# Scalar-tensor-tensor in place of tensor-tensor for three vector operations of a routing stage

## The reference

```python
def _L0_ffn_ref(hidden_states, rms_w, gate_w, w13, w2, sw_gate, sw_up, sw_down):
    H, I, E, K, CAP = 256, 128, 64, 2, 256
    x = _rmsnorm(hidden_states, rms_w).reshape(-1, H)
    logits = x @ gate_w.T
    topk_w, topk_ids = top_k(softmax(logits), K)
    topk_w = topk_w / sum(topk_w)
    ... # sort the 2T choices by expert, at most CAP per expert in its buffer
    xb = buf[:, :CAP]
    g, u = split(einsum('ech,ehf->ecf', xb, w13))
    yb = einsum('eci,eih->ech', silu(g) * u, w2)
    moe_out = ...  # weighted rows back to their tokens
    shared = silu(x @ sw_gate) * (x @ sw_up) @ sw_down
    return moe_out + shared + residual

x = x + 0.5 * ffn(layernorm(x))
x = x + attn(layernorm(x))     # MLPs of width 1024, causal mixing of 1024 tokens
x = x + 0.5 * ffn(layernorm(x))
```

## Time and profile before

| what | value |
|---|---|
| three timed runs | 2141.43, 2149.87, 2153.97 us (median 2149.87) |
| the profiled execution | 2137.34 us, its span 2135.6 us |
| granted TensorE clock, mean | 0.977 of full speed |
| busy share of the span: PE, DVE, ACT, POOL | 92%, 62%, 51%, 52% |
| stage `dispatch`: start of its last VectorE operation (L496) | 189.19 us |

### The profile page before, as it was taken

The page is one execution under the profiler, slowest core; times in us unless marked ns, Lnnn a source line. Parts: engine busy times, 40 slices in busy tenths (PEclk is TensorE's granted clock), DMA queues, the critical chain, the costliest instruction groups (busy, mean ns, idle before and its releaser), DMA issues.

```text
span 2135.6 us, 32644 instructions
## 1 busy us (share of the span) xinstructions
PE 1970.7 (92%) x11134; PEld 1676.3 (78%) x11134; DVE 1319.4 (62%) x3475; ACT 1084.4 (51%) x1989; POOL 1117.6 (52%) x1251
## 2 busy tenths in 40 slices
PE   6996899599999999999999999999999977898987
PEld 4665888578888888888888888888888865788854
DVE  5996666455566576576575575665665543555568
ACT  6873666444445455454454454454454534455652
POOL 5875667353255546545645645545545326466610
PEclk9998999899999999999999999999999989999998
DMA  8434899790032022121220210110100302688787
GB/s 283 150 119 144 276 295 299 251 308 27 1 99 80 21 99 65 36 94 35 70 87 23 89 40 21 60 40 21 60 11 21 126 11 70 220 276 304 277 281 270
DMA packets 236407, 270.09 MB, mean 126 GB/s; under 512 B 25489, under 2 KB 186322, under 8 KB 236242
## 3 DMA queue, kind: packets, MB, share of 16 engines
q1 hardware_dynamic: 207570, 200.79, 29.0%
q0 software_dynamic: 28672, 67.22, 9.5%
HBM read 150.35 MB, written 117.57 MB: 125 GB/s over the span
## 4 chain that ended last, share of the span: by engine, by line
PE 66%; DVE 6%; issue 3%; ACT 3%; POOL 1%; another core or an unknown queue 1%; DMA 0%; ACTq 0%; DVEq 0%; POOLq 0%
PE attention_ring L1997 22%; PE attention_acc L2027 14%; PE attention_acc L2017 8%; PE attention_acc L2264 3%; PE attention_acc L2252 2%; DVE attention_hid_l L1712 2%; PE attention_work L2090 2%; PE attention_ring L2252 2%; PE attention_work L2110 2%; PE attention_work L2106 2%; PE attention_work L2073 2%; PE attention_ring L2206 2%; PE attention_ring L2239 1%; PE attention_work L1985 1%; PE attention_work L2047 1%
## 5 line engine op out<-in xcount | busy, mean ns | idle before, releaser
L1712 DVE TENSOR_TENSOR attention_hid_l<-attention_gelu,attention_hid_h 128x512 fp32r<-128x512 f32 x384 | 286.0, 745 | 467.6 <-ACT attention_gelu L1351 270.1
L1348 ACT ACTIVATE attention_hid_h<-attention_ring,home_b 128x512 fp32r<-128x512 f32 x384 | 264.3, 688 | 540.3 <-PE attention_ring L1997 475.7
L1351 ACT ACTIVATE attention_gelu<-attention_ring,home_b 128x512 f32<-128x512 f32 x384 | 261.7, 682 | 0.0
L1997 PE MATMUL attention_ring<-attention_n_t_h,home_w_h 128*128 128x512 f32 x512 | 204.0, 398 | 1.6 <-DVE attention_n_t_l L1704 1.6
L2027 PE MATMUL attention_acc<-attention_hid_h,home_w_h 128*128 128x512 f32 x512 | 201.2, 393 | 2.9 <-DVE home_room L1729 1.3
L1997 PE MATMUL attention_ring<-attention_n_t_h,home_w_l 128*128 128x512 f32 x512 | 199.8, 390 | 0.0
L2027 PE MATMUL attention_acc<-attention_hid_l,home_w_h 128*128 128x512 f32 x512 | 199.6, 390 | 0.0
L1997 PE MATMUL attention_ring<-attention_n_t_l,home_w_h 128*128 128x512 f32 x512 | 199.5, 390 | 0.0
L2027 PE MATMUL attention_acc<-attention_hid_h,home_w_l 128*128 128x512 f32 x512 | 199.3, 389 | 0.0
L1190 POOL DMA_INDIRECT home_room<-expert_rows,routing_slots x128 | 139.0, 1086 | 93.9 <-issue 54.1
L1326 POOL DMA_INDIRECT token_rows<-home_room,attention_gelu x128 | 128.7, 1005 | 99.0 <-ACT home_room L1447 64.2
(11 more groups left out here) (309 smaller groups left out, 5259.6 us busy)
## 6 DMA issues: line engine op xcount, KB each, us to landing
experts_w<-in_L_ffn_w SPq DMA_DIRECT2D x64, 256.0 KB
expert_rows<-experts_y SPq DMA_DIRECT2D x64, 256.0 KB
slot_rows<-const_zeros SPq DMA_DIRECT2D x16, 1024.0 KB
token_rows<-const_zeros SPq DMA_DIRECT2D x16, 1024.0 KB
home_room<-in_L_ffn_w SPq DMA_DIRECT2D x64, 256.0 KB
home_room<-slot_rows SPq DMA_DIRECT2D x64, 256.0 KB
final_y_rows<-token_rows SPq DMA_DIRECT2D x32, 512.0 KB, 6.5
dispatch_x_in<-in_L_attn_x SPq DMA_DIRECT2D x16, 512.0 KB, 5.6
```

What stands on the lines that cost most here:

```text
L1348: act.activation(hid[n % PARTS][0][:, :], ring[n % RING][:, :], ACT.Gelu, bias=b1[:, m, c:c + 1])
L1351: act.activation(gelu[n % GELUS][:, :], ring[n % RING][:, :], ACT.Gelu, bias=b1[:, m, c:c + 1]).then_inc(ring_free, 1)
L1712: dve.tensor_tensor(hid[n % PARTS][1][:, :], gelu[n % GELUS][:, :], hid[n % PARTS][0][:, :].bitcast(fp32), ALU.subtract).then_inc(hid_read ...
L1997: last = pe.matmul(ring[n % RING][:, :], w1[m][wp][:, k, c * P:(c + 1) * P], rows_t[xp][:, k, :], start=(q == 0), stop=(q == 2 * len(TERMS ...
```

## The change

Three operations of `choose` take the form scalar-tensor-tensor, which computes (first tensor op scalar) op second tensor:

- the gap: (best x -1.0) + second, in place of second - best;
- `chosen`: (expert number x 1.0) is equal to choice. This form takes tensors of at most two free dimensions here, so the one instruction of 512 elements becomes a loop of two with 256 each, one per k; the second signals `chosen_done`;
- `either`: (marks of k = 0 x 1.0) + marks of k = 1.

```diff
--- before.py
+++ after.py
@@ -414,7 +414,7 @@
                 for t in range(GT):
                     dve.wait_ge(max_done, GT * g + t + 1)
                     dve.max_index(top8_at[s][:, t, :], top8[s][:, t, :], ps_logits[:, t, :]).then_inc(index_done, 1)
-                dve.tensor_tensor(gap_all[:, now], top8[s][:, :, 1], top8[s][:, :, 0], ALU.subtract).then_inc(gap_ready, 1)
+                dve.scalar_tensor_tensor(gap_all[:, now], top8[s][:, :, 0], -1.0, top8[s][:, :, 1], ALU.mult, ALU.add).then_inc(gap_ready, 1)
                 dve.wait_ge(index_done, GT * (g + 1))
                 dve.tensor_copy(expert_all[:, :, now], top8_at[s][:, :, 0:2].rearrange("p t k -> p k t")).then_inc(expert_done, 1)
                 if g >= F:
@@ -423,11 +423,14 @@
                     dve.wait_ge(places_ready, g - F + 1)
                     dve.wait_ge(carried, g - F + 2)
                 dve.wait_ge(expert_done, g + 1)
-                dve.tensor_tensor(
-                    chosen[s][:, :, :, :], iota_e[:, :].unsqueeze(1).unsqueeze(1).broadcast_to(full),
-                    expert_all[:, :, now].unsqueeze(3).broadcast_to(full), ALU.is_equal).then_inc(chosen_done, 1)
+                of = [P, GT, EXPERTS]
+                for k in range(2):
+                    last = dve.scalar_tensor_tensor(
+                        chosen[s][:, k, :, :], iota_e[:, :].unsqueeze(1).broadcast_to(of), 1.0,
+                        expert_all[:, k, now].unsqueeze(2).broadcast_to(of), ALU.mult, ALU.is_equal)
+                last.then_inc(chosen_done, 1)
                 dve.wait_ge(chosen_done, g + 1)
-                dve.tensor_tensor(either[s][:, :, :], chosen[s][:, 0, :, :], chosen[s][:, 1, :, :], ALU.add).then_inc(either_ready, 1)
+                dve.scalar_tensor_tensor(either[s][:, :, :], chosen[s][:, 0, :, :], 1.0, chosen[s][:, 1, :, :], ALU.mult, ALU.add).then_inc(either_ready, 1)
 
             def places_at(g):
```

## The result

| | median | lowest to highest | runs |
|---|---|---|---|
| kernel before | 2152.28 us | 2141.43 to 2159.11 | 20 |
| kernel after | 2155.72 us | 2151.08 to 2163.22 | 20 |

The ratio of the runs is 1.0022 with a 95% interval of 1.0012 to 1.0032. On 2152 us that is 4.7 us more, between 2.6 and 6.9 (the two medians are 3.4 us apart): real, small, and within the 0.5% that was called no change.

A forecast was written before the change was run, and what follows sets the result against it. VectorE, waiting on GpSimd's L294, was taken to set the dispatch period; `chosen` 0.08 plus `either` 0.14 gave 0.22 us, times 13 groups 2.9 us, on 2149.87 giving 2152.8 us, range 2140 to 2163.

The forecast's parts named there:

- What bounds the stage: Dispatch stage: the loop L406, GpSimd's chain to L294's end, cast, `chosen`, `either`, statistics sets the 10.09 us period.
- 0.69 us of air: Dispatch stage: TensorE, busy 9.40 us of each 10.09 us period, lets the period fall by 0.69 us at most.
- The gap: nothing: Gap subtraction (L417): the new form also waits for L294, 2.1 us of wait hiding its cost; +0.00 us per group.
- `chosen`: +0.08: `chosen` in dispatch: two overlapping operations of 256 elements take 0.78 us against 0.69 for one; +0.08 us per group.
- `either`: +0.14: `either` in dispatch: the new form on bf16 goes at fp32 pace, 428 ns against 292; +0.14 us per group.
- 13 groups: Dispatch stage: only groups 1 to 13 pay 0.22 us each, 2.9 us together; groups 0, 14 and 15 absorb it.
- The sign that was named: Dispatch stage's end: the last VectorE instruction comes about 3 us later than before (189.19).
- Rival A: Gap in dispatch: the new form does not wait for GpSimd, gap 0.15 us, total 2142.4 us; chance 0.12.
- Rival B: `chosen` and `either`: the new form streams at half pace, 0.69 us per 256 elements, total 2163.6 us; chance 0.04.

The follow-up runs named there:

- dose experiment: Kernel after with `either` computed twice, the first time into a tile nobody reads; period 10.627 us, +0.33 over the kernel after.
- nearly empty L294: Kernel after with GpSimd's shared-expert addition L294 cut to one column of each tile; period 9.032 us, total 2065.65 us beside 2081.44.
- plain split: Kernel before with `chosen` split into two plain tensor-tensor operations of 256 elements; period 10.158 us, +0.07.
- reordered kernel with the variances later: Kernel before with GpSimd's big operations right after the counts, VectorE's statistics at round end, variances behind MAX8 and FIND_INDEX8; 2140.5 us, ratio 0.9938.
- kernel with the gaps at the end: Kernel before with all groups' gaps computed in one subtraction after the last group; period 10.009 us, ratio 0.9998.

## Why the prediction was right

*What bounds the stage.* Right. The loop from L406 over GpSimd's chain, cast, `chosen`, `either` and the statistics sets the period; the dose experiment shows no slack in it, and the nearly empty L294 shows what lies beneath. Only the distance to the next bound was wrong: TensorE had not 0.69 us of air in a period but 1.06.

*The gap: nothing.* Right. It starts 0.11 us behind L294 and ends with it, in either form; its place in the period is 0.00. The reading of the earlier trace rows, that a form which keeps GpSimd out is itself kept out, held: in the kernel after, and again in L485 of its second trace (2.47 us in place of 0.29). The section on the chip says that the engines meet only at semaphores; these waits, of operations that have already started, are meetings of another kind.

*`chosen`: +0.08.* Measured +0.07. The prediction gave it to two operations in place of one, and the plain split confirms that the form has no part in it. 423 ns against 428 from the slope of the earlier trace rows.

*`either`: +0.14.* Measured +0.13. The new form on bf16 goes at the pace of fp32, 425 ns. Here the Trainium skill's list of forms with a packed pace (Vector Engine (DVE) Microarchitecture Reference, section 5.1), which leaves this one out, agrees with the run.

*13 groups.* Right for the middle: each interval between the `either` of groups 1 to 14 grows by about 0.2 us, and the last one stays at 9.30. 13 x 0.204 = 2.65 us, where 2.9 was forecast. Whether group 0 absorbs its share can't be seen under the scatter of the start. Group 15 doesn't always absorb it: at full clock 0.44 us came on behind its `either`, at the lower one 0.21 fell away. The sign that was named, the stage's last VectorE operation about 3 us later, came out at 2.72 and 2.68. The totals' 4.7 us (2.6 to 6.9) hold that. Whether there is more in the total, and whether the lower clock at the end is part of it, is open. The time itself was forecast as 2152.8 from a base of 2149.87; the base came out at 2152.28, and the growth is what counts: +0.13% forecast, +0.22% measured (0.12 to 0.32).

*Rival A was mis-sized.* It didn't happen, but its price was wrong, in two steps. The first: that with a gap that does not wait VectorE would be free. With the gap out of the loop the cast, which the change leaves as it is, waited 2.15 us for L294 in its place, and the period fell by 0.08. So the rival would have given next to nothing. The second: "the period can fall by 0.69 at most", from TensorE's 9.40 busy us. Freed of the wait, the period fell by 1.06, and came to 9.03 to 9.08 in three kernels in which VectorE had 8.2 to 8.4 us of work. The text had 8.3 us at most, rather 7.5, for the whole freeing; the reordered kernel with the variances later was 13 us faster by its ratio. Its sentence that even so large a freeing would stay under 0.5% doesn't hold well either: the ratio's 0.6% has an interval of 0.4% to 0.85%.

*Rival B* fell: 423 ns, not 690. The Trainium skill's sentence on half throughput with two non-bf16 sources (same page, section 7, Points that are easy to get wrong) is not borne out by the fp32 row. The new rows can't judge it: `chosen` and `either` have at most one fp32 tensor, and the gap, with two, has only four elements (145 ns at its shortest).

## What to carry to other kernels

Before rewriting an operation that looks dear, see what its time is made of: the gap's 2.26 us were GpSimd's, and neither form of it could give them back. Nor could its removal, since the next operation took the wait over. A tensor-tensor with all operands in bf16 should keep that form; with an fp32 operand the scalar-tensor-tensor costs the same, and splitting one operation in two costs about 0.07 us. Where VectorE and GpSimd take turns, put GpSimd's operations on large tiles beside VectorE's statistics, MAX8 or PSUM reads, and check one-input SBUF operations as well. And don't take an engine's busy time for the time that it needs.

## What was not expected of the hardware

- One-input operations of 4 and 8 elements from SBUF to SBUF waited for a GpSimd operation to its end: a cast for 2.15 us, a variance operation for 1.80, in place of about 0.16. MAX8, FIND_INDEX8 and the statistics did not.
- GpSimd's L261, with 8 elements, kept nothing out in its 1.71 us; L294, with 1024, did.
- TensorE's busy time isn't its need: 9.40 us in a period of 10.09, 9.03 in one of 9.03, for the same matmuls of nearly the same lengths, which overlap more.
- The product of 8 matmuls at the stage's end took 1.97 us in five traces and 2.48 to 3.65 in nine, at granted clocks of 1.00 and of 0.53 to 0.76, after 2.4 to 2.5 us of idleness in nearly all of them.
- The kernel before took about 2150 us in some comparisons and 2081 in others; why isn't known. Where can be seen: set against the first trace of before (span 2135.6 us), that of the kernel with the gaps at the end (2079.9) is level at the first gather (191.50 and 191.07), 18 us ahead near 400 us, still 18 near 1600, and 56 at the end. So the difference arises before 450 us and after 1700 us, where the experts of the two routed layers run, which no edit here touches.
